# Another order of the weight preparation among the steps of a first attention layer

## The reference

```python
def ternary_quant(w_fp32, g=GROUP_SIZE):            # GROUP_SIZE = 64
    w = w_fp32.astype(jnp.bfloat16)
    w_g = w.reshape(-1, g)
    scale = jnp.clip(jnp.mean(jnp.abs(w_g), axis=-1, keepdims=True), 1e-08, None)
    q = jnp.clip(jnp.round(w_g / scale), -1, 1)
    w_hat = (q * scale).reshape(w.shape)
    return w + jax.lax.stop_gradient(w_hat - w)
...
gu = jnp.einsum('bsd,hd->bsh', x, ternary_quant(w_gate_up))
gate, up = jnp.split(gu, 2, axis=-1)
h = jax.nn.silu(gate) * up
hn = rms_norm(h)
return jnp.einsum('bsh,dh->bsd', hn, ternary_quant(w_proj))
...
x = x + s * g        # s: attention of layernorm(x), g: silu of the net's result
```

## Time and profile before

| | |
|---|---|
| median of 3 runs | 830.03 us (829.26 to 830.63) |
| the profiled execution | 829.26 us, its span 827.5 us |
| busy over the span | TensorE 94%, VectorE 74%, ScalarE 57%, GpSimd 36% |
| granted TensorE clock, mean | 0.979 |

### The profile page before, as it was taken

One profiled execution on the slowest core, in us unless ns is written; L12 is line 12 of the kernel. 1 busy time (PEld: TensorE's weight loads), 2 busy tenths in 40 slices (PEclk: granted clock), 3 DMA queues, 4 the chain that ended last, 5 costly groups with the idle time before them and its releaser, 6 DMA issues.

```text
span 827.5 us, 13259 instructions
## 1 busy us (share of the span) xinstructions
PE 774.2 (94%) x4608; PEld 478.4 (58%) x4608; DVE 613.6 (74%) x1644; ACT 474.1 (57%) x962; POOL 295.0 (36%) x255
## 2 busy tenths in 40 slices
PE   4877968989999999999999999999999999999996
PEld 2554656836436667856446667865545667774533
DVE  6969786778857677787957677787976667778862
ACT  3796755253786766133795765243686766233483
POOL 1258651032006886001104887101102988200201
PEclk9989889999999999999999999999999999999998
DMA  9131002076003120039001310028101310007400
GB/s 301 54 91 45 1 27 82 1 202 181 3 2 97 46 59 8 1 109 242 9 2 46 84 59 20 1 78 252 30 2 32 85 33 1 2 36 231 91 3 26
DMA packets 56819, 55.37 MB, mean 67 GB/s; under 512 B 14257, under 2 KB 43313, under 8 KB 56753
## 3 DMA queue, kind: packets, MB, share of 16 engines
q1 hardware_dynamic: 52768, 49.63, 21.0%
q10 hardware_dynamic: 3664, 3.84, 1.7%
q0 software_dynamic: 320, 1.05, 0.4%
HBM read 39.00 MB, written 15.24 MB: 66 GB/s over the span
## 4 chain that ended last, share of the span: by engine, by line
PE 69%; DVE 11%; issue 11%; ACT 5%; POOL 2%; DMA 1%; ACTq 0%; POOLq 0%; DVEq 0%
PE bank L929 13%; PE bank L1040 6%; PE bank L1247 5%; PE bank L1231 5%; PE bank L964 5%; PE bank L1142 5%; PE bank L1026 5%; PE bank L1170 4%; PE bank L1214 3%; PE bank L1007 3%; PE bank L975 2%; PE bank L1219 2%; PE bank L1162 2%; PE bank L989 2%; ACT region L764 1%
## 5 line engine op out<-in xcount | busy, mean ns | idle before, releaser
L1605 DVE TENSOR_REDUCE mx<-bank 128x1 f32<-128x512 f32 x256 | 161.2, 686 | 27.6 <-PE bank L1170 22.7
L605 POOL TENSOR_TENSOR region<-region 128x512 f32<-128x512 f32 x75 | 99.9, 1332 | 148.1 <-DVE region L1423 143.4
L929 PE MATMUL bank<-xnT,wrope 128*128 128x512 f32 x320 | 147.4, 603 | 2.6 <-ACT xnT L734 1.6
L879 ACT ACTIVATE region<-bank 128x512 f32<-128x512 f32 x256 | 132.9, 602 | 25.7 <-PE bank L1219 24.2
L764 ACT ACTIVATE region<-region,nb 128x128 f32<-128x128 f32 x256 | 81.5, 390 | 69.3 <-DVE nb L1435 69.2
L929 PEld LDWEIGHTS bank<-xnT,wrope 128*128 128x128 f32 x320 | 58.7, 194 | 64.9 <-issue 60.3
L601 POOL TENSOR_TENSOR region<-region,sin_sb 128x512 f32<-128x512 f32 x60 | 79.8, 1330 | 42.6 <-ACT region L747 42.0
L634 POOL TENSOR_TENSOR region<-region,bo_bc 128x256 f32<-128x256 f32 x16 | 11.6, 728 | 204.0 <-DVE region L1484 204.0
L1416 DVE TENSOR_TENSOR region<-bank,cos_sb 128x512 f32<-128x512 f32 x80 | 54.3, 686 | 34.1 <-PE bank L929 33.8
L964 PE MATMUL bank<-region 128*128 128x128 f32 x512 | 76.1, 295 | 3.3 <-POOL region L605 1.7
L745 ACT ACTIVATE region<-bank 64x512 f32<-64x512 f32 x80 | 47.5, 594 | 49.0 <-DVE region L1416 39.6
(11 more groups left out here) (144 smaller groups left out, 1341.0 us busy)
## 6 DMA issues: line engine op xcount, KB each, us to landing
wrope<-in_wrope SPq DMA_DIRECT2D x80, 128.0 KB, 2.2
scratch<-region SPq DMA_DIRECT2D x16, 512.0 KB, 5.0
Qp<-scratch SPq DMA_DIRECT2D x56, 128.0 KB, 3.6
Kp<-scratch SPq DMA_DIRECT2D x56, 128.0 KB, 3.7
scratch<-region SPq DMA_DIRECT2D x16, 256.0 KB, 5.8
X<-in_x SPq DMA_DIRECT2D x4, 512.0 KB, 4.1
out<-X SPq DMA_DIRECT2D x16, 128.0 KB, 1.9
VW<-v_rows SPq DMA_DIRECT2D x16, 102.0 KB, 2.7
```

The lines of the kernel that those rows point to most:

```text
L605: nc.gpsimd.tensor_tensor(dst, dst, tiles(sw[:, r % 2, :], i), ALU.add)\
L879: nc.scalar.activation(P1[:, n % 8, :], turned_bank(n)[:, :], ACT.Exp, scale=SCALE1)\
L929: mm = nc.tensor.matmul(misc(b, name)[:, 0:width], lhs(c), xnT[:, c, :], start=(c == 0), stop=(c == DC - 1))
L1605: nc.vector.tensor_reduce(mx1[:, g % 2, column:column + 1], scores_bank(m)[:, :], AX.X, ALU.max)\
```

## The change

VectorE's 30 steps are grouped otherwise and stand elsewhere. Each piece has now two portions: scales with k = 0 and 1, and k = 2, 3 and 4. The first portions of pieces 1 to 5 stand in units 0, 3, 5, 8 and 10, the second ones in units 1, 4, 6, 9 and 11, and both stand behind `gate` and `times_up` of their unit. On ScalarE `turned_weights` (units 2, 7 and 12) and the copy `turned_outputs(b, 0)` (unit 15) stand ahead of `first_blocks(s - 1)` of their unit. TensorE, GpSimd and SyncE have the same order as before, and nothing changes for VectorE in batches 1 to 3.

```diff
--- before.py
+++ after.py
@@ -117,15 +117,8 @@
 OT_UNIT = NKV * TT - 1
 FFN_FIRST = [0, 0, 0, 2, 1, 1, 2, 2, 2, 1, 1, 1, 1, 2, 0, 0]
 PREPARED = {1: 2, 3: 3, 6: 4, 8: 5}
-TERN_STEPS = (2, 2, 2, 2, 2, 3, 3, 2, 2, 2, 3, 3, 2, 0, 0, 0)
-
-
-def ternary_at(s):
-
-    first = sum(TERN_STEPS[:s])
-    return [(1 + k // 6, k % 6) for k in range(first, first + TERN_STEPS[s])]
-
-
+TERN_FIRST = {0: 1, 3: 2, 5: 3, 8: 4, 10: 5}
+TERN_SECOND = {1: 1, 4: 2, 6: 3, 9: 4, 11: 5}
 SPLIT_AT = {13: ((0, 0),), 14: ((0, 1), (1, 0)), 15: ((1, 1),)}
 TURN_UNITS = (2, 7, 12)
 FFN_LATER = [0, 0, 2, 2, 0, 0, 2, 2, 0, 0, 2, 2, 2, 1, 1, 0]
@@ -820,12 +813,12 @@
                         for kind, i in ffn_at(b, s):
                             if kind == "gate":
                                 half_tanh(b, i)
+                        for k in range(2) if b == 0 and s in TURN_UNITS else ():
+                            turned_weights(2 * TURN_UNITS.index(s) + k)
+                    if s == OT_UNIT:
+                        turned_outputs(b, 0)
                     if b == 0 and s:
                         first_blocks(b, s - 1)
-                    for k in range(2) if b == 0 and s in TURN_UNITS else ():
-                        turned_weights(2 * TURN_UNITS.index(s) + k)
-                    if s == OT_UNIT:
-                        turned_outputs(b, 0)
                     if b == 0 and s in PREPARED:
                         prepare(PREPARED[s])
                     for n, k in SPLIT_AT.get(s, ()) if b == 0 else ():
@@ -1519,13 +1512,15 @@
                             times_cos(b, r)
                     if b and 1 <= s <= NKV * TT:
                         first_blocks(b, s - 1)
-                    for n, step in ternary_at(s) if b == 0 and s < NKV * TT else ():
-                        if step == 0:
-                            scales(n)
-                        else:
-                            quantise(n, step - 1)
                     for kind, i in ffn_at(b, s) if s < NKV * TT else ():
                         (gate if kind == "gate" else times_up)(b, i)
+                    if b == 0 and s in TERN_FIRST:
+                        scales(TERN_FIRST[s])
+                        for k in range(2):
+                            quantise(TERN_FIRST[s], k)
+                    if b == 0 and s in TERN_SECOND:
+                        for k in range(2, 5):
+                            quantise(TERN_SECOND[s], k)
                     for n, k in SPLIT_AT.get(s, ()) if b == 0 else ():
                         split_ffn1(n, k)
                     if s >= TT + 1 and (s - TT - 1) % TT == 0:
```

## The result

The changed kernel takes 844.21 us (843.04 to 846.29), against 830.33 us (829.26 to 830.78) for the kernel before on the same chip: a ratio of 1.0172, with a 95% interval of 1.0154 to 1.0191. The forecast was 844.5 us. Its profiled execution took 843.55 us.

The account below looks back on a forecast made before the run. VectorE was taken to set the pace in batch 0's units 5 to 12, with TensorE waiting. VectorE's idle time of 9.7 us plus 4.8 us beside GpSimd, on 830.0, gave 844.5 us; 8-in-10 range 836 to 850.

Parts of the forecast that it names:

- The gaps: VectorE idles before gates in batch 0, awaiting half_tanh: 1.4 to 2.6 us each in units 6, 7, 8, 9, 11.
- Units 0 to 4: Through gate 1: late mask(1) delays ScalarE, and a quantise step moved behind gate; 1.4 to 2.4, taken as 1.9 us.
- Unit 7: Batch 0, unit 7: a 1.4 us gap before gate 3, hidden by an earlier VectorE wait; nothing added or won.
- mask(12) behind piece 5: Unit 12's mask now follows piece 5's end, so the transposes waiting for that piece gain 0.8 us.
- Beside GpSimd: VectorE's quantise steps in batch 0 meet GpSimd operations more often and lengthen; 0 to 7.4, taken as 4.8 us.
- The sign that all five means would be 0.1 to 0.3 us higher: VectorE's quantise lines, k = 0 to 4, should each show a mean duration higher by 0.1 to 0.3 us.
- The forecast's own range: Total time 841 to 848 us, with gaps 9.2 to 10.2 and GpSimd 1.5 to 7.4 us; chance 0.56.
- What hides the rest: ScalarE's reordering costs nothing, turned_weights give 0.5 us back early; later batches have no moved instruction.
- Gaps alone: GpSimd met no oftener, or ScalarE shorter than reckoned: 839.7 us, or 835.5 with two gaps filled; chance 0.22.
- Every step meets GpSimd: Every step that can meets GpSimd, and TensorE stays longer at its lower clock: 847.1, up to 850 us; chance 0.15.
- Faster: Piece 1's last step and turned_weights come sooner, if masks can be late without cost: 827.1 us; chance 0.04.
- No change: Late masks fall into TensorE's own idle time and the order evens out by unit 12: 830.0 us; chance 0.03.

Follow-up runs that it names:

- `q1_back`: The changed kernel with k = 1 of piece 1 moved back behind unit 1's mask and cos steps: 841.49 us, ratio 1.0135.
- short pair: The kernel before and the changed kernel, both with batch 0's GpSimd operations cut to 32 of 512 columns: 821.61 and 830.52 us.
- `act_only`: The kernel before with only ScalarE's part of the change: 831.10 us, ratio 1.0003.
- `dve_only`: The changed kernel with ScalarE's order as before, so VectorE's part of the change alone: 845.94 us, ratio 1.0180.
- `unit9_ahead`: The changed kernel with k = 2 to 4 of piece 4 in unit 9 laid ahead of gate 5: 844.60 us, ratio 1.0167.

## Why the prediction was right

The mechanism stood in the main, and the sum of 14.5 us met 13.9. The single terms were less good than their sum: two were some 2 us too small each, and two others 1.1 and 2.9 us too large.

- **The gaps.** Forecast 2.0, 1.4, 2.6, 2.6 and 1.4 us for units 6, 7, 8, 9 and 11. The gates' waits are 2.03, 1.26, 1.97, 2.66 and 1.26. Four are within 0.2 us. Unit 8's is shorter since TensorE's rotary products held up VectorE's cos steps there, in the time in which ScalarE caught up.
- **Units 0 to 4, mis-sized.** Forecast 1.4 to 2.4 us, of it 0.2 to 1.2 for ScalarE's lateness. Gate 1 ran at 65.80 and not at 63.26, 2.5 us later, and k = 2 behind it adds its 1.2: 3.8. The lateness was too small in the sum. mask(1) came 1.87 late (40.04 against 38.17), since k = 1 took its long form (1.63). ScalarE's copies of the weights were still 1.4 us late (50.13 against 48.76), and so were TensorE's first gate products. These took 3.62 us and not 2.46 at the lower granted clock, and ScalarE's first_blocks(2), behind them, ran 2.5 us late (56.21 against 53.67), as did all of ScalarE from there to gate 1. So 1.2 of the 2.5 us are TensorE's lower clock, which the sum had at nothing. `q1_back` confirms the place.
- **Unit 7, wrong.** I had it hidden: 3.6 us against 3.8. From the end of piece 3 (88.69 + 1.63 = 90.32) to mask(8) at 96.13 it was 5.8, 2.0 us more. The row at 93.27 names what I had missed: the second weight transpose of that pair waited 1.85 us for gate 3, because it writes into the PSUM bank that holds gate 3's product. The gap before gate 3 went to TensorE by way of a bank.
- **mask(12) behind piece 5.** The -0.8 holds by the order: mask(12) starts at 133.80, right behind k = 4 at 133.19.
- **Beside GpSimd.** Forecast 4.8. The five lines rose from 31.9 to 36.9 us, by 5.0. By the timelines 16 of the 25 steps were lengthened, and 12 before; I had counted 17. What I left out are other instructions that meet GpSimd: the two small ones of scales fell from 5.9 to 4.7 us, and the last one of outputs0 (L1472 before) from 1.8 to 0.9. The net is 2.9. One us of it lies in piece 1 and is part of mask(1)'s lateness. The short pair gives 4 to 5 us, give or take 3, so it can't tell 4.8 from 2.9. That a step and a GpSimd operation hold each other up is seen in the timelines at 66.41 to 69.36. The sign that all five means would be 0.1 to 0.3 us higher came for k = 0 and 4; k = 1 and 3 rose by more, and k = 2 fell from 1.61 to 1.31. The forecast's own range took 1.5 us as the least for this part, where its working named 0 as the bound.
- **The sum after the fact.** 3.8 + 2.0 + 2.0 (unit 7) + 1.5 (unit 8, whose two waits for rotary products shrank by 0.4) + 2.7 + 1.3 - 0.8 + 1.9 = 14.4, at transposes that came 13.9 later. That the forecast total was closer than its terms is luck: 3.9 us of missing terms stood against 1.1 us too much in unit 8 and some 2.9 too much beside GpSimd.
- **What hides the rest.** ScalarE's order alone costs and brings nothing that can be told (`act_only`); beside VectorE's new order the trace of `dve_only` gives it 2.2 us, where the forecast had 0.5. Behind the transposes the time was the same, 707.8 us against 707.4.
- **The rivals.** "Gaps alone" (839.7) was refuted as a total, and its 9.7 us are 8.9 in the short pair. "Every step meets GpSimd" was too much, net; that TensorE is at its lower clock for longer came true (0.82 from 64 to 135 us, against 0.87), and in unit 3 it cost 1.2 us of the path. "Faster" needed masks that can be late: the exps' waits doubled. "No change" needed free time in VectorE: it made itself new idle time of 16.5 us at the gates.

## What to carry to other kernels

When an engine works for another one in a loop (VectorE's mask, ScalarE's chain, VectorE's gate), independent work belongs between what feeds the chain and what waits for it. Laid behind the waiting instruction, the same work leaves the engine idle for the rest of the chain and then delays the next round. How finely it was cut hardly mattered here; where it stood did. A wait that seems hidden should be followed through the buffers of the waiting product, too, and the granted clock of the products behind a new wait should be read before a microsecond is put down to order alone.

## What the runs showed of the hardware

- The same block of 16 products (128x128 by 128x256) took 3.70 us in the kernel before and the changed one, and 5.39 us in `unit9_ahead`, with a mean granted clock of 1.00 and 0.69. TensorE's instructions there stand in the same order in all three, and in each of them it had stood idle twice not long before, for 1.0 to 2.5 us. A gain of 2.5 us ahead of it was thus followed by a loss of 1.7. Why the clock was lower in the one trace isn't shown. Small gains before such a place can't be judged by the total of one kernel.
- The first four pairs of gate products took 2.14 us in `q1_back` at a granted clock of 1.00, after 1.02 us of idle time, and 3.62 us in the changed kernel at 0.54, after 1.72 us of it.
- VectorE's steps with two SBUF operands and GpSimd's operations alternate when both have work queued, each step then being up to about 1.0 us longer than its short form (0.69 to 1.64 for k = 3 and 4). Seen at 66.41 to 69.36 in the changed kernel.
